# Another order of the on-chip buffers in an attention and feed-forward kernel

## The chip, the core and the metric

The kernel runs on one core of a Trainium2 chip. The metric is the device time of one execution in microseconds (us). SBUF, the on-chip memory, has 128 partitions, and a buffer takes the same bytes in each of them; "place" below always means a byte offset within a partition.

## The reference, cut to what matters

```python
xn = layernorm(x)                              # x: 8 batches x 2048 tokens x 256
q, k, v = split(xn @ Wqkv + bqkv)
qp, kp = elu(q) + 1, elu(k) + 1
kv = kp.T @ v ; ksum = sum(kp, tokens)         # per batch
attn = (qp @ kv) / (qp @ ksum + 1e-6)
z = layernorm(xn + attn) * g1 + b1
ffn = (silu(z @ Wg + bg) * (z @ Wu + bu)) @ Wd + bd     # hidden width 682
s = layernorm(z + ffn) * g2 + b2
out = x + s * silu(xn @ ternary(W).T * scale)
```

## The kernel before, in words

The tokens are cut into 32 groups of 512 (`TOK`), four tiles of 128 rows each. A program of one loop iteration per group is written out by hand for each engine (`TENSOR_JOBS`, `SCALAR_STEPS`, `VECTOR_STEPS`, `GPSIMD_STEPS`, and their fill and end forms); keys-values work runs up to five groups ahead of the feed-forward work, and semaphores alone tie the engines together. SyncE issues all transfers.

Most products are made in three parts (`parts3`): each operand is held as a high half and a low half (`_h`, `_l`, type fp32r), and high by high, low by high and high by low are added up in PSUM. Each product is one weight load of 128x128 (the left operand, L1278 and the helper `products`) and one pass of the right operand, the moving one, 512, 258 or 256 columns wide. The kinds that matter:

| job | weights (left) | moving (right) | columns |
|---|---|---|---|
| G, U, GU (`gate_or_up`) | `wgu_h`, `wgu_l` | `zT_h`, `zT_l` | 512 |
| Q | `wqk_h`, `wqk_l` | `xT_h`, `xT_l` | 512 |
| D (`Dn`), parts of h | `h_h`, `h_l` | `wd_h`, `wd_l` | 256 |
| D, last part | `ht` | `wd_h` | 256 |
| K | `xT_h`, `xT_l` | `wqk_h`, `wqk_l` | 256 |
| B | `xT_h`, `xT_l` | `tern` | 256 |
| XK | `xn_h`, `xn_l` | `kp_h`, `kp_l` | 256 |
| KV | `kv_h`, `kv_l` (as `xk_h`, `xk_l`) | `wv_h`, `wv_l` | 256 |
| N | `qp_h`, `qp_l` | `kv_h`, `kv_l` | 258 |
| warm | `ht` | `ht` | 512 |

The profile prints the moving operand and the weights of a row in alphabetical order, so that `bank<-kv_h,qp_h` is N with the weights `qp_h`. The warm products fill idle time at the start and are used by nothing.

The buffers are declared one after another (`sb(...)`), and each starts at the first multiple of 32 bytes behind the one before it; `ident`, the first, starts at a multiple of 128. So the five small buffers behind it and the small vectors and statistics further on decide where the large ones start. Steps within a buffer (chunks, tiles, 128 columns) are multiples of 512 bytes, except in `kv_h` and `kv_l`, whose two rows are `KVW` = 258 elements, 1032 bytes, long. Places of the operands modulo 128, worked out from the declarations:

| buffers | place modulo 128 before |
|---|---|
| `wqk_*`, `tern`, `wgu_*`, `wd_*`, `wv_*`, `xn_*`, `xT_*`, `kp_*` | 32 |
| `kv_h`: first row, second row | 32, 40 |
| `kv_l`: first row, second row | 64, 72 |
| `qp_h`, `qp_l` | 96 |
| `zT_*`, `h_*`, `ht` | 64 |

Of the kernel before, what the change touches and what calls it, by code (L numbers as in the profile page):

```python
# [211 lines left out]
def build_kernel(nc, x, wqkv, bqkv, wg, bg, wu, bu, wd, bd, g1, b1, g2, b2, wt, out):  # L212
# [10 lines left out]
    with ctx:  # L223
        def sb(name, shape, dt=f32):
            return ctx.enter_context(nc.sbuf_tensor(name, shape, dt))
# [3 lines left out]


        ident = sb("ident", [P, P])
        ones = sb("ones", [P, 1])
        one_zero = sb("one_zero", [P, 2])
        neg_half = sb("neg_half", [P, 1])
        less_h = sb("less_h", [P, 1])
        less_w = sb("less_w", [P, 1])

        wqk_h = sb("wqk_h", [P, DC, 2 * D], f32r)
        wqk_l = sb("wqk_l", [P, DC, 2 * D], f32r)
        tern = sb("tern", [P, DC, D], f32r)  # L240
# [3 lines left out]
        wd_h = sb("wd_h", [P, HC, D], f32r)  # L244
        wd_l = sb("wd_l", [P, HF, D], f32r)
        wv_h = sb("wv_h", [P, DC, D], f32r)
        wv_l = sb("wv_l", [P, DC, D], f32r)
        bvb = sb("bvb", [P, D])
        bk1b = sb("bk1b", [P, D])
        bq = sb("bq", [P, DC])  # L250
        bq1 = sb("bq1", [P, DC])
        nbq = sb("nbq", [P, DC])
        g1c = sb("g1c", [P, DC])
        b1c = sb("b1c", [P, DC])
        hb = sb("hb", [P, 2 * HC])
        hb0 = sb("hb0", [P, 2 * HC])
        hb1 = sb("hb1", [P, 2 * HC])
        tscale = sb("tscale", [P, 4])
# [6 lines left out]
        xn_h = sb("xn_h", [P, TILES, D], f32r)  # L265
        xn_l = sb("xn_l", [P, TILES, D], f32r)
        xT_h = sb("xT_h", [P, XT, DC, TOK], f32r)
        xT_l = sb("xT_l", [P, XT, DC, TOK], f32r)
        st = sb("st", [P, 3, TILES, 6])
        mv = sb("mv", [P, 3, TILES, 2])  # L270
        ve = sb("ve", [P, 3, TILES])
        rstd0 = sb("rstd0", [P, LN0, TILES])
        nmr0 = sb("nmr0", [P, LN0, TILES])
        kp = sb("kp", [P, KP, 2, D])
        ku = sb("ku", [P, KU, 2, D])
        kp_h = sb("kp_h", [P, TILES, D], f32r)
        kp_l = sb("kp_l", [P, TILES, D], f32r)
        ksum = sb("ksum", [P, 2, D])
        kv_h = sb("kv_h", [P, DC, KVW], f32r)
        kv_l = sb("kv_l", [P, DC, KVW], f32r)  # L280

        xq = sb("xq", [P, 3, TILES, D])
        qp = sb("qp", [P, DC, TOK])
        qp_h = sb("qp_h", [P, DC, TOK], f32r)
        qp_l = sb("qp_l", [P, DC, TOK], f32r)
        den = sb("den", [P, 2, 2])
        rstd1 = sb("rstd1", [P, TILES])
        nmr1 = sb("nmr1", [P, TILES])
# [4 lines left out]

        hs = sb("hs", [P, 2, TOK])
        h_h = sb("h_h", [P, HRING, TOK], f32r)
        h_l = sb("h_l", [P, HRING, TOK], f32r)

        ht = sb("ht", [P, TOK], f32r)  # L300
        norm2 = sb("norm2", [P, 2, TILES])
# [45 lines left out]
        def job_bank(kind, g, n):  # L347
            return bank[NUMBER[kind, g, n] % RING]
# [199 lines left out]
        def _(eng):  # L548
# [140 lines left out]
            for i in ITERATIONS:  # L689
                a, q, f, last = i + LEAD, i + 1, i, i - 1  # L690
                run_steps(order_of(i, FILL_GPSIMD, GPSIMD_STEPS, END_GPSIMD), {
                    "at": i,                    "xn_low": (a, xn_low), "sum_k": (a, sum_k), "z_g1": (f, z_g1), "tail_again": (f, tail_again), "last_gain": (last, last_gain), "last_offset": (last, last_offset),
                    "last_gate": (last, last_gate), "last_add": (last, last_add),
                    "end_terms": (f, end_terms),
                    "a_rstd": (a + 1, lambda g, p: first_rstd(p) if g == 0 else rstd(0, g, rstd0[:, g % LN0, :])),
                    "q_rstd": (q, lambda g, _: rstd(1, g, rstd1[:, :])),
                    "last_rstd": (last, lambda g, _: rstd(2, g, rstd2[:, :])), "setup_d_low": (a, setup_d_low), "setup_masks": (a, setup_masks)})


# [1 line left out]
        def _(eng):  # L701
# [223 lines left out]
        def _(eng):  # L925
# [348 lines left out]
        def _(eng):  # L1274
# [213 lines left out]
```

## Time and profile before

| | |
|---|---|
| median of 3 runs | 1224.95 us (1224.54 to 1226.43) |
| the profiled execution | 1226.01 us, span 1224.3 us |
| TensorE busy | 98% of the span |
| VectorE busy | 88% of the span |
| ScalarE busy | 78% of the span |
| GpSimd busy | 69% of the span |
| TensorE's granted clock, mean | 0.998 |

PE is TensorE's matmuls, PEld its weight loads, DVE VectorE, ACT ScalarE, POOL GpSimd. A matmul's duration in a row includes its way through the array, which overlaps the next one, so the time that a product takes of the engine is the distance from its start to the start of the next.

### The profile page before, as it was taken

The numbers are of one execution on the slowest core, as the hardware profiler recorded it, in microseconds if no ns is written. First come the engines' busy times: TensorE is split into PE (matmuls) and PEld (weight loads), VectorE is DVE, ScalarE is ACT, GpSimd is POOL, SyncE is SP. The second block draws the span as 40 slices with busy tenths as digits, with TensorE's granted clock in tenths as the row PEclk, the third lists the DMA queues.
The fourth block names the chain that finished last, engine by engine and source line by source line (L and its number), as shares of the span: only waits on it lengthen the run. The fifth ranks groups of instructions, "written<-read, shape, count | busy, mean of one in ns | idle before, by whom it ended". The sixth has DMA issues, their size and how long they took to land.

```text
span 1224.3 us, 24021 instructions
## 1 busy us (share of the span) xinstructions
PE 1205.6 (98%) x7550; PEld 1080.2 (88%) x7550; DVE 1081.3 (88%) x2467; ACT 953.4 (78%) x1557; POOL 842.6 (69%) x994
## 2 busy tenths in 40 slices
PE   8999999999999999999999999999999999999997
PEld 6889988999988999988999988999988999888886
DVE  6988999999999999999999999999999999777765
ACT  7787888777888777888778888778887778767753
POOL 3443787667687676787757787677776777666676
PEclk9999999999999999999999999999999999999999
DMA  7213432234432234432334432244432233222201
GB/s 215 76 46 87 121 105 69 87 104 121 122 103 70 87 105 121 121 104 70 86 104 120 116 109 70 72 119 122 121 95 58 94 118 104 69 70 67 73 18 35
DMA packets 137523, 115.61 MB, mean 94 GB/s; under 512 B 12339, under 2 KB 122293, under 8 KB 137398
## 3 DMA queue, kind: packets, MB, share of 16 engines
q1 hardware_dynamic: 137398, 114.08, 31.9%
q8 instruction: 62, 1.02, 0.3%
q14 instruction: 63, 0.52, 0.1%
HBM read 67.38 MB, written 46.67 MB: 93 GB/s over the span
## 4 chain that ended last, share of the span: by engine, by line
PE 90%; DVE 4%; issue 2%; DMA 1%; ACT 1%; POOL 1%; SPq 0%; DVEq 0%; POOLq 0%; ACTq 0%
PE bank L1278 64%; PE d_bank L1278 18%; PE xk_bank L1278 8%; DVE st L930 1%; DMA xa<-z_turned 1%; PE bank L1292 1%; DMA z_turned<-xa 1%; DVE rz L1062 0%; DVE zT_l L1093 0%; ACT rz L703 0%; DVE h_l L1113 0%; SPq L452 0%; DVE xa L1082 0%; POOL rstd L577 0%; ACT h_h L703 0%
## 5 line engine op out<-in xcount | busy, mean ns | idle before, releaser
L1278 PE MATMUL bank<-zT_h,wgu_h 128*128 128x512 f32 x704 | 278.5, 396 | 0.3 <-DVE rz L1062 0.3
L1278 PE MATMUL bank<-zT_l,wgu_h 128*128 128x512 f32 x704 | 278.5, 396 | 0.0
L1278 PE MATMUL bank<-zT_h,wgu_l 128*128 128x512 f32 x704 | 278.4, 395 | 0.0
L1278 PE MATMUL d_bank<-wd_h,h_h 128*128 128x256 f32 x640 | 180.6, 282 | 0.0
L1278 PE MATMUL d_bank<-wd_l,h_h 128*128 128x256 f32 x640 | 180.1, 281 | 0.0
L1278 PE MATMUL d_bank<-wd_h,h_l 128*128 128x256 f32 x640 | 180.1, 281 | 0.0
L1103 DVE SCALAR_TENSOR_TENSOR bank<-bank,hb,hs 128x512 f32<-128x512 f32 x160 | 118.2, 754 | 54.5 <-ACT hs L703 41.8
L1278 PEld LDWEIGHTS bank<-zT_l,wgu_h 128*128 128x128 f32 x704 | 132.3, 188 | 31.4
L703 ACT ACTIVATE h_h<-bank 128x512 fp32r<-128x512 f32 x160 | 95.7, 598 | 81.4 <-DVE bank L1103 81.3
L1278 PEld LDWEIGHTS bank<-zT_h,wgu_h 128*128 128x128 f32 x704 | 132.4, 188 | 25.9 <-DVE rz L1062 1.3
L1278 PEld LDWEIGHTS bank<-zT_h,wgu_l 128*128 128x128 f32 x704 | 132.9, 189 | 23.6
L703 ACT ACT_TABLE_LOAD x116 | 148.8, 1283 | 4.0 <-POOL wd_l L686 1.2
L703 ACT ACTIVATE hs<-bank,hb 128x512 f32<-128x512 f32 x192 | 128.1, 684 | 29.5 <-PE bank L1278 29.1
L600 POOL TENSOR_TENSOR ksum<-ksum,kp 128x256 f32<-128x256 f32 x120 | 107.7, 898 | 46.4 <-DVE kp L1029 43.1
L577 POOL TENSOR_TENSOR norm<-ve,neg_half 128x4 f32<-128x4 f32 x32 | 32.7, 1023 | 150.8 <-DVE ve L941 150.8
L1113 DVE TENSOR_TENSOR h_l<-bank,h_h 128x512 fp32r<-128x512 f32 x160 | 109.9, 687 | 23.7 <-ACT h_h L703 18.4
L703 ACT ACTIVATE rz<-rz,norm 128x256 f32<-128x256 f32 x124 | 74.2, 600 | 63.1 <-DVE norm L1139 63.1
L1278 PEld LDWEIGHTS d_bank<-wd_h,h_l 128*128 128x128 f32 x640 | 120.6, 189 | 2.8
L1278 PEld LDWEIGHTS d_bank<-wd_h,h_h 128*128 128x128 f32 x640 | 120.0, 187 | 3.4 <-DVE h_l L1113 0.5
L1278 PEld LDWEIGHTS d_bank<-wd_l,h_h 128*128 128x128 f32 x640 | 120.7, 189 | 0.0
L650 POOL TENSOR_TENSOR rz<-rz,g1b 128x256 f32<-128x256 f32 x128 | 117.4, 928 | 0.0
L610 POOL TENSOR_TENSOR rz<-rz,g2b 128x256 f32<-128x256 f32 x124 | 90.4, 739 | 34.9 <-ACT rz L703 34.9
(165 smaller groups left out, 3682.2 us busy)
## 6 DMA issues: line engine op xcount, KB each, us to landing
xq<-in_L_attn_x_dram SPq DMA_DIRECT2D x32, 512.0 KB, 5.9
xa<-in_L_attn_x_dram SPq DMA_DIRECT2D x31, 512.0 KB, 3.8
out_dram<-rz SPq DMA_DIRECT2D x31, 512.0 KB, 5.0
z_turned<-xa SPq DMA_DIRECT2D x120, 128.0 KB, 3.4
xa<-z_turned SPq DMA_DIRECT2D x30, 512.0 KB, 4.2
turned<-xa SPq DMA_DIRECT2D x108, 128.0 KB, 2.4
xa<-turned SPq DMA_DIRECT2D x27, 512.0 KB, 3.9
rz<-in_L_attn_Wg_dram SPq DMA_DIRECT2D x1, 640.0 KB, 5.7
```

The lines of the kernel that those rows point to most:

```text
L577: eng.tensor_tensor(dst, ve[:, k, :], neg_half[:, 0:1].to_broadcast([P, TILES]), ALU.pow).then_inc(S[f"rs{k}"], 1)
L600: eng.tensor_tensor(ksum[:, slot, :], ksum[:, slot, :], part, ALU.add).then_inc(S["ks"], 1)
L610: eng.tensor_tensor(row_, row_, g2b[:, :], ALU.mult).then_inc(S["a"], 1)
L650: eng.tensor_tensor(row_, row_, g1b[:, :], ALU.mult).then_inc(S["zg"], 1)
L703: return eng.activation(out_, in_, func, **kw).then_inc(S[name], 1)
L930: eng.bn_stats(st[:, k, t, :], rows).then_inc(S[f"bn{k}"], 1)
L1103: eng.scalar_tensor_tensor(out=hidden(g, c)[0:rows, :], in0=up, scalar=hb[0:rows, HC + c:HC + c + 1], in1=hs[0:rows, n % 2, :], op0=ALU.ad ...
L1113: eng.tensor_tensor(h_l[:, slot, :], hidden(g, c)[:, :], h_h[:, slot, :].bitcast(f32), ALU.subtract).then_inc(S["hl"], 1)
L1278: ins = eng.matmul(dst, left, right, start=first and n == 0, stop=last and n == len(pairs) - 1, **kw)
L1292: ins = eng.transpose(dst[:, c * D + t * P:c * D + (t + 1) * P], src[:, 2 * p + t, c * P:(c + 1) * P], ident[:, :])
```

## The change

The declarations are put into another order. The small buffers that split the large ones are gathered into a few (`consts`, `masks`, `norm1`, `vecs`) behind the operands, and views with the old names are cut from them. The rows of `kv_h` and `kv_l` get eight more elements than `D` instead of two, those of `qp_h` and `qp_l` eight more than `TOK`, and every use names the old width. Two small buffers, `hb` and `hb0`, stand between the halves of kv and of qp. No instruction is added, removed or moved in its engine's order, and no semaphore changes.

```diff
+SHIFT = 8
         ident = sb("ident", [P, P])
-        ones = sb("ones", [P, 1])
-        one_zero = sb("one_zero", [P, 2])
-        neg_half = sb("neg_half", [P, 1])
-        less_h = sb("less_h", [P, 1])
-        less_w = sb("less_w", [P, 1])
...
         wqk_h = sb("wqk_h", [P, DC, 2 * D], f32r)
         wqk_l = sb("wqk_l", [P, DC, 2 * D], f32r)
         tern = sb("tern", [P, DC, D], f32r)
+        wd_h = sb("wd_h", [P, HC, D], f32r)
+        wd_l = sb("wd_l", [P, HF, D], f32r)
+        kp_h = sb("kp_h", [P, TILES, D], f32r)
+        kp_l = sb("kp_l", [P, TILES, D], f32r)
+        kv_h = sb("kv_h", [P, DC, D + SHIFT], f32r)
+        hb = sb("hb", [P, 2 * HC])
+        kv_l = sb("kv_l", [P, DC, D + SHIFT], f32r)
+        xT_h = sb("xT_h", [P, XT, DC, TOK], f32r)
+        xT_l = sb("xT_l", [P, XT, DC, TOK], f32r)
+        h_h = sb("h_h", [P, HRING, TOK], f32r)
+        h_l = sb("h_l", [P, HRING, TOK], f32r)
+        ht = sb("ht", [P, TOK], f32r)
+        zT_h = sb("zT_h", [P, DC, TOK], f32r)
+        zT_l = sb("zT_l", [P, DC, TOK], f32r)
+        xn_h = sb("xn_h", [P, TILES, D], f32r)
+        xn_l = sb("xn_l", [P, TILES, D], f32r)
+        wv_h = sb("wv_h", [P, DC, D], f32r)
+        wv_l = sb("wv_l", [P, DC, D], f32r)
         NGU = (2 * HF + 1) * P
         wgu_h = sb("wgu_h", [P, DC, NGU], f32r)
         wgu_l = sb("wgu_l", [P, DC, NGU], f32r)
+        qp_h = sb("qp_h", [P, DC, TOK + SHIFT], f32r)
         hb0 = sb("hb0", [P, 2 * HC])
+        qp_l = sb("qp_l", [P, DC, TOK + SHIFT], f32r)
...
-                act(kv_h[:, c, :], job_bank("KV", g, c)[:, 0:KVW], ACT.Copy, "kvh")
+                act(kv_h[:, c, 0:KVW], job_bank("KV", g, c)[:, 0:KVW], ACT.Copy, "kvh")
...
-                    for pair in parts3(qp_h[:, c, s], qp_l[:, c, s], kv_h[:, c, :], kv_l[:, c, :])], "N")
+                    for pair in parts3(qp_h[:, c, s], qp_l[:, c, s], kv_h[:, c, 0:KVW], kv_l[:, c, 0:KVW])], "N")
```

Places modulo 128 after, by the same rule:

| buffers | place modulo 128 after |
|---|---|
| `wqk_*`, `tern`, `wd_*`, `kp_*` | 0 |
| `kv_h`, `kv_l`: first row, second row | 0, 32 |
| `xT_*`, `h_*`, `ht`, `zT_*`, `xn_*`, `wv_*`, `wgu_*` | 64 |
| `qp_h`, `qp_l`: first row, second row | 64, 96 |
| `bvb` and all behind it (`xa`, `xn`, `kp`, `ku`, `ksum`, `xq`, `qp`, `rz`, `sg`, `hs`) | 64 |

## Rows read from the trace of the kernel before

**Rows 1.** The page: span, and busy time of each engine over it.
```profile
span 1224.3 us, 24021 instructions
PE 1205.6 (98%) x7550; PEld 1080.2 (88%) x7550; DVE 1081.3 (88%) x2467; ACT 953.4 (78%) x1557; POOL 842.6 (69%) x994
```

**Rows 2.** Busy time by stretch: window, length, PE, PEld, DVE, ACT, POOL, clock, DMA.
```profile
200.00:1000.00 800.00, 799.90 (x5091) 723.41 (x5090) 742.31 (x1663) 653.03 (x1061) 585.82 (x673) 1.00 0.35 102
```

**Rows 3.** The chain that ended last, its longest pieces: start, length, what.
```profile
240.20 2.88 PE d_bank L1278 x24
...
368.86 18.84 PE bank L1278 x106
405.24 18.84 PE bank L1278 x106
```

**Rows 4.** Waits from 200 to 1000 us: total, times, longest.
```profile
DVE bank L1103 <- ACT hs L703: 27.1, 22, 1.4
...
PEld bank L1278 <- DVE h_l L1113: 1.0, 4, 0.5
```

**Rows 5.** Groups of PE's matmuls by form: count | busy us, mean ns | idle before.
```profile
L1278 PE MATMUL bank<-zT_l,wgu_h 128*128 128x512 f32 x704 | 278.5, 396 | 0.0
...
L1278 PE MATMUL d_bank<-wd_h,h_h 128*128 128x256 f32 x640 | 180.6, 282 | 0.0
...
L1278 PE MATMUL bank<-kv_h,qp_h 128*128 128x258 f32 x256 | 74.2, 290 | 1.7 <-DVE kv_l L1180 1.7
L1278 PE MATMUL bank<-wqk_h,xT_h 128*128 128x256 f32 x256 | 73.3, 286 | 0.1
...
L1278 PE MATMUL bank<-tern,xT_l 128*128 128x256 f32 x256 | 63.8, 282 | 0.0
...
L1278 PE MATMUL xk_bank<-kp_l,xn_h 128*128 128x256 f32 x224 | 63.3, 282 | 0.0
...
L1278 PE MATMUL bank<-xT_h,wqk_h 128*128 128x512 f32 x128 | 50.7, 396 | 0.1
...
L1278 PE MATMUL d_bank<-wd_h,ht 128*128 128x256 f32 x128 | 21.2, 287 | 0.0
```

**Rows 6.** Timeline of PE within one iteration: start us, duration us, what.
```profile
405.07 0.28 PE L1278 MATMUL bank<-wqk_h,xT_h 128*128 128x256 f32 x1
...
406.50 0.28 PE L1278 MATMUL bank<-kv_h,qp_h 128*128 128x258 f32 x1
...
406.85 0.30 PE L1278 MATMUL bank<-kv_h,qp_h 128*128 128x258 f32 x1
406.98 0.29 PE L1278 MATMUL bank<-kv_h,qp_l 128*128 128x258 f32 x1
...
409.43 0.39 PE L1278 MATMUL bank<-zT_h,wgu_h 128*128 128x512 f32 x1
...
416.45 0.28 PE L1278 MATMUL bank<-tern,xT_h 128*128 128x256 f32 x1
...
417.40 0.40 PE L1278 MATMUL bank<-zT_h,wgu_h 128*128 128x512 f32 x1
...
418.79 0.39 PE L1278 MATMUL bank<-xT_h,wqk_h 128*128 128x512 f32 x1
...
421.57 0.28 PE L1278 MATMUL bank<-tern,xT_h 128*128 128x256 f32 x1
```

**Rows 7.** Timeline of PE at two places of the fill: the warm products, merged.
```profile
12.64 1.29 PE L1278 MATMUL bank<-ht 128*128 128x512 f32 x5
...
69.13 0.85 PE L1278 MATMUL bank<-ht 128*128 128x512 f32 x3
69.82 0.28 PE L1278 MATMUL xk_bank<-kp_h,xn_h 128*128 128x256 f32 x1
```

**Rows 8.** DVE groups by form: count | busy us, mean ns | idle before, releasers.
```profile
L1113 DVE TENSOR_TENSOR h_l<-bank,h_h 128x512 fp32r<-128x512 f32 x160 | 109.9, 687 | 23.7 <-ACT h_h L703 18.4
...
L999 DVE TENSOR_TENSOR xT_l<-xa,xT_h 128x512 fp32r<-128x512 f32 x54 | 36.5, 676 | 0.0
```

More of the change, by code:

```diff
@@ L243, in build_kernel @@
         wgu_l = sb("wgu_l", [P, DC, NGU], f32r)
[L244 to L247, printed above, removed]
+        qp_h = sb("qp_h", [P, DC, TOK + SHIFT], f32r)
+        hb0 = sb("hb0", [P, 2 * HC])
+        qp_l = sb("qp_l", [P, DC, TOK + SHIFT], f32r)
+        hb1 = sb("hb1", [P, 2 * HC])
+        consts = sb("consts", [P, 4])
+        masks = sb("masks", [P, 2])
+        norm1 = sb("norm1", [P, 2, TILES])
+        norm2 = sb("norm2", [P, 2, TILES])
+        den = sb("den", [P, 2, 2])
+        tscale = sb("tscale", [P, 4])
+        vecs = sb("vecs", [P, 5, DC])
+        st = sb("st", [P, 3, TILES, 6])
+        mv = sb("mv", [P, 3, TILES, 2])
+        ve = sb("ve", [P, 3, TILES])
+        rstd0 = sb("rstd0", [P, LN0, TILES])
+        nmr0 = sb("nmr0", [P, LN0, TILES])
         bvb = sb("bvb", [P, D])
         bk1b = sb("bk1b", [P, D])
[L250 to L258, printed above, removed]
         g1b = sb("g1b", [P, D])
@@ L264, in build_kernel @@
         xn = sb("xn", [P, TILES, D])
[L265 to L273, printed above, removed]
         kp = sb("kp", [P, KP, 2, D])
         ku = sb("ku", [P, KU, 2, D])
-        kp_h = sb("kp_h", [P, TILES, D], f32r)
-        kp_l = sb("kp_l", [P, TILES, D], f32r)
         ksum = sb("ksum", [P, 2, D])
-        kv_h = sb("kv_h", [P, DC, KVW], f32r)
-        kv_l = sb("kv_l", [P, DC, KVW], f32r)
         xq = sb("xq", [P, 3, TILES, D])
         qp = sb("qp", [P, DC, TOK])
[L284 to L288, printed above, removed]
         rz = sb("rz", [P, RZ, TILES, D])
-        zT_h = sb("zT_h", [P, DC, TOK], f32r)
-        zT_l = sb("zT_l", [P, DC, TOK], f32r)
         sg = sb("sg", [P, SG, TILES, D])
         hs = sb("hs", [P, 2, TOK])
[L295 to L301, printed above, removed]
+        ones, one_zero, neg_half = consts[:, 0:1], consts[:, 1:3], consts[:, 3:4]
+        bq, bq1, nbq, g1c, b1c = (vecs[:, n, :] for n in range(5))
+        less_h, less_w = masks[:, 0:1], masks[:, 1:2]
+        rstd1, nmr1 = norm1[:, 0, :], norm1[:, 1, :]
         rstd2, nmr2 = norm2[:, 0, :], norm2[:, 1, :]
@@ L695, in _ @@
                     "a_rstd": (a + 1, lambda g, p: first_rstd(p) if g == 0 else rstd(0, g, rstd0[:, g % LN0, :])),
-                    "q_rstd": (q, lambda g, _: rstd(1, g, rstd1[:, :])),
+                    "q_rstd": (q, lambda g, _: rstd(1, g, rstd1)),
                     "last_rstd": (last, lambda g, _: rstd(2, g, rstd2[:, :])), "setup_d_low": (a, setup_d_low), "setup_masks": (a, setup_masks)})
@@ L776, in q_high @@
                     eng.wait_ge(S["N"], TILES * g)
-                act(qp_h[:, c, :], qp[:, c, :], ACT.Copy, "qph")
+                act(qp_h[:, c, 0:TOK], qp[:, c, :], ACT.Copy, "qph")
             def x_res(g, t):
@@ L1049, in q_low @@
                 eng.wait_ge(S["qph"], DC * g + c + 1)
-                eng.tensor_tensor(qp_l[:, c, :], qp[:, c, :], qp_h[:, c, :].bitcast(f32),
+                eng.tensor_tensor(qp_l[:, c, 0:TOK], qp[:, c, :], qp_h[:, c, 0:TOK].bitcast(f32),
                                   ALU.subtract).then_inc(S["qpl"], 1)
@@ L1071, in attn_norm @@
                     eng.wait_ge(S["z"], TILES * g)
-                eng.scalar_tensor_tensor(out=nmr1[:, :], in0=mv[:, 1, :, 0], scalar=-1.0,
-                                         in1=rstd1[:, :], op0=ALU.mult, op1=ALU.mult).then_inc(S["nm1"], 1)
+                eng.scalar_tensor_tensor(out=nmr1, in0=mv[:, 1, :, 0], scalar=-1.0,
+                                         in1=rstd1, op0=ALU.mult, op1=ALU.mult).then_inc(S["nm1"], 1)
             def z_turn(g, _=0):
@@ L1179, in kv_low @@
                     eng.wait_ge(S["kvh"], DC * (g // GPB) + c + 1)
-                    eng.tensor_tensor(kv_l[:, c, :], job_bank("KV", g, c)[:, 0:KVW],
-                                      kv_h[:, c, :].bitcast(f32), ALU.subtract).then_inc(S["kvl"], 1)
+                    eng.tensor_tensor(kv_l[:, c, 0:KVW], job_bank("KV", g, c)[:, 0:KVW],
+                                      kv_h[:, c, 0:KVW].bitcast(f32), ALU.subtract).then_inc(S["kvl"], 1)
             def setup_bk():
```

## The prediction

> **What bounds the kernel now.** The page comes first: TensorE is busy for 98% of the span, VectorE, the next, for 88% [rows 1]. An average hides stages, so the middle was read as a stretch of its own: between 200 and 1000 us TensorE is busy for 799.90 of 800 us, VectorE for 742.31 [rows 2]. The clock there is the full one (1.00, 2.4 GHz) in that same row. The chain of waits agrees: its long pieces are TensorE's, and the same piece comes back after 405.24 - 368.86 = 36.38 us, one iteration [rows 3]. TensorE hardly waits for anyone (1.0 us in those 800, [rows 4]). So the time is the number of products by the distance between their starts, and what is to be asked is whether the places of the operands set that distance.
>
> The timeline gives the distances [rows 6]. K: 12 products from 405.07 to 406.50, 119 ns each. N: 24 from 406.50 to 409.43, 122 ns. G and U: 30 from 409.43 to 416.45, 234 ns. B: 8 from 416.45 to 417.40, 119 ns. Q: 12 from 418.79 to 421.57, 232 ns. D: 24 in 2.88 us, 120 ns [rows 3].
>
> **The change part by part.** Nothing is issued that was not issued before, so no instruction, wait or transfer has a price of its own. What can change is the distance between products, and the duration of other engines' instructions.
>
> *Gate and up products.* Before, their weights stand at 32 and z at 64 (modulo 128); after, both at 64. The trace has products of the same width and type with both operands at 64: the warm ones. Five of them take 1.29 us, and taking off the last one's 0.39 leaves four distances in 0.90, 225 ns, by rounding 223 to 227 [rows 7, 6]. In the second place three warm products stand before a product of XK, whose weights are at 32: 69.13 to 69.82 is 230 ns each [rows 7], between the two values, as it should be if a load of weights at 32 beside a stream at 64 is what costs. I take 227, the upper end. Against it: the warm products load the same weights again and again, early in the fill. Bounds: 0 (234 stays) and 9 ns (225). There are 3 x 704 products [rows 5], so 2112 x 7 = 14.8 us. A loss is not excluded by any mechanism that I know; the nearest price for one is N's below.
>
> *N.* Its distances are not equal: the one from 406.85 to 406.98 is 130 ns, against 117 (406.50 to 406.85 is three products) [rows 6]. The long distances, two of each six, have the second row of `kv_h` as the moving operand, which begins 8 bytes behind a multiple of 32; after, it begins at 32. The 3 x 256 products [rows 5] hold 256 of that kind, and 256 x 9 ns is 2.3 us. If the first rows, at 0 beside weights at 64, gain what the next paragraph takes for its products, that is 384 x 6 = 2.3 us more. Sum 4.6.
>
> *The 256-wide products (D, K, B, XK, KV).* Before, every moving operand stands at 32; the weights at 32, or 64 in D, and the distance is 119 to 120 either way [rows 3, 6]. After, the moving operand is at a multiple of 64 in all and the weights too, but 64 bytes apart modulo 128. No row shows a 256-wide product with both at multiples of 64. Upper bound: the cost goes with the columns, and half of 227 is 113.5, a gain of 6. Lower bound: nothing (119.5 stays), or, on the other side, N's 130, a loss of 10. I take 6, from the warm products, the only rows in which both operands are so placed. The count is 3 x 640 + 128 (D), 3 x 256 (K), 2 x 256 (B), 3 x 224 (XK) [rows 5], 4000: 24 us. KV's are few and left out.
>
> *Q.* 3 x 128 products [rows 5] go from 32 and 32 to weights at 0, x at 64. From 232 to 227 is 5 ns, 1.9 us; bounds 0 and 7 ns.
>
> A rule of the Trainium skill speaks against these terms: "SBUF — State Buffer", note on SBUF "cachelines" in the section on the DMA port swizzle, has lines of 16 bytes, and by those every operand here but the second rows of kv already starts on a line. Then N's 2.3 us would be all. The trace doesn't side with it: starts at 32 and at 64 are both on such lines, and 234 stands against 225 [rows 6, 7].
>
> *The other engines.* Their buffers move too, mostly from 32 or 96 to 64. VectorE's low half of h, with operands at 64, takes 687 ns, and that of x, at 32, 676 [rows 8]; so they cost 0, with 11 ns either way as the bound. These are two of about 75 instructions in an iteration (1663 in 800 us, [rows 2]); 11 ns on 20 long ones would be 0.2 us of an engine that has room.
>
> **What is late next.** Sum of TensorE's terms: 14.8 + 4.6 + 24 + 1.9 = 45.3 us, over 32 groups about 1.4 us each, from some 36.9 (one iteration in four is longer by the keys-values work: 800 us hold 21.7). VectorE is busy for 742.31 / 21.7 = 34.2 us of these 36.9. With 35.5 it would have 1.3 us of idle time left, where it now waits 1.2 us an iteration (27.1 / 21.7) for ScalarE's silu alone [rows 2, 4]. Those waits hang on TensorE's products and move forward with them, but not all of them will fit: in an order written out by hand, some product will find its operand late. I give back a quarter, 11 us. A gain of 34 us on the profiled execution's 1226.01 gives 1192; it stood 1 us above the median of the runs, so 1191 against 1224.95.
>
> **The rivals.**
> - *Only the gate and up products gain* (and N's second rows): the 256-wide ones and Q stay because for so short a stream the load of the next 128 columns of weights is as long as the stream. For it: D, with weights at 64, is no faster than K with 32 [rows 3, 6]. Against: no row has such a product's moving operand at 64. 14.8 + 2.3 = 17 us, no idle time of VectorE used up: 1208.
> - *VectorE takes over earlier*: half of the 45 us is given back, 1203.
> - *The places don't matter*: warm products are quick because they reload the same weights, not for their place. For it: G with weights at 32 (234) and Q with its moving operand at 32 (232) are nearly alike. Left is N's 2.3 us, 1222.6, which is 0.19%. This is also the rule on lines of 16 bytes.
> - *Slower*: weights 64 bytes from the stream clash with it. This holds for all 256-wide products after. At the price of N's long distances (10 ns) it costs 40 us on 4000 products, less the 14.8 of gate and up and 2.3: 1248. It decides from about 4 ns a product (17.1 us / 4000). Against: N's first three products are 64 apart in two of three (`qp` at 96, `kv_h` at 32) and take 117 ns.
>
> **How the numbers follow.** Forecast (both widths gain) 50%, its own range 1180 to 1200; only gate and up 22%; VectorE takes over 10%; places don't matter 10%; slower 8%. The two next cases lie at 1203 and 1208, with some 6 us about them for unknown sizes, so 1178 to 1214 holds the first three less their edges, 8 in 10. Faster by over 0.2% (2.4 us, about what a measurement of this kernel can tell from no change): the first three and a share of the fourth, 85%; within it 7%; slower 8%.
>
> **What would show it.** Distances in the timeline of the changed kernel: G and U at 227 instead of 234; K, B, D and XK at 113 to 114 instead of 119; all N products alike, none at 130; VectorE's busy share in 200 to 1000 us at 95% or more, and small waits of TensorE on VectorE. If G and U stay at 234 the first term is wrong, and with it the reading of the warm products; if K and D stay at 119 the first rival holds; if TensorE's products are as said and the iteration is longer than 36 us, VectorE took over.

## The result, and the profile after

The kernel after takes 1212.78 us (median of 4 runs, 1211.86 to 1213.07), the kernel before 1225.42 beside it: ratio 0.9897, 95% interval [0.9881, 0.9912]. It is faster by 12.6 us, where the prediction had 34; the time lies inside the range. The profiled execution took 1213.05 us. Of all executions told below, one, the profiled one of `by32`, was disturbed (3042.83 us); it is left out of that kernel's time, and the kernel has no row in the table.

The page's span and busy times, and the middle as one stretch (window, length, PE, PEld, DVE, ACT, POOL, clock, DMA), answer to [rows 1, 2]:
```profile
span 1211.3 us, 24021 instructions
PE 1191.9 (98%) x7550; PEld 1069.5 (88%) x7550; DVE 1081.7 (89%) x2467; ACT 952.8 (79%) x1557; POOL 843.9 (70%) x994
```
```profile
200.00:1000.00 800.00, 799.88 (x5127) 723.31 (x5126) 749.92 (x1687) 657.26 (x1069) 593.21 (x680) 1.00 0.35 102
```
TensorE still bounds it: full clock, busy for all of the 800 us, but 5127 products start in that time instead of 5091. VectorE does the same work (1081.7 us against 1081.3) in less time.

The chain (start, length, what) has the pieces of [rows 3], 18.57 us for 18.84 and 2.83 for 2.88, and a period of 583.22 - 547.33 = 35.89 us for 36.38:
```profile
237.43 2.83 PE d_bank L1268 x24
...
547.33 18.57 PE bank L1268 x106
583.22 18.57 PE bank L1268 x106
```

The timeline of PE in one iteration (start, duration), for [rows 6]:
```profile
401.11 0.28 PE L1268 MATMUL bank<-wqk_h,xT_h 128*128 128x256 f32 x1
...
402.53 0.28 PE L1268 MATMUL bank<-kv_h,qp_h 128*128 128x258 f32 x1
...
405.40 0.40 PE L1268 MATMUL bank<-zT_h,wgu_h 128*128 128x512 f32 x1
...
406.79 0.42 PE L1268 MATMUL bank<-zT_h,wgu_h 128*128 128x512 f32 x1
407.06 0.40 PE L1268 MATMUL bank<-zT_h,wgu_l 128*128 128x512 f32 x1
407.29 0.39 PE L1268 MATMUL bank<-zT_l,wgu_h 128*128 128x512 f32 x1
407.52 0.39 PE L1268 MATMUL bank<-zT_h,wgu_h 128*128 128x512 f32 x1
```
K: 12 products in 1.42 us, 118 ns each. N: 24 in 2.87, 120. In G and U one distance is 270 ns (406.79 to 407.06), the next two 230. A single series proves little, so the means over the whole kernel are needed.

The table below has them, for this kernel and for the experiments told further on. From the starts of all products in the timeline the distance to the next start was taken, sorted by kind; distances over 250 ns (512 columns), 140 (258) or 135 (256) were counted apart as waits, with what they exceed 230, 120 or 119 ns by. "Sum" is the mean of each kind times its count: 2112 G and U, 384 Q, 2048 D, 768 K, 512 B, 672 XK, 768 N, and 96 KV, which have no column of their own.

| kernel | G/U | Q | D | K | B | XK | N | sum, us | waits: count, us |
|---|---|---|---|---|---|---|---|---|---|
| before | 233.3 | 231.8 | 119.7 | 118.7 | 119.0 | 119.1 | 122.0 | 1164.3 | 59, 9.9 |
| **after** | 229.4 | 233.4 | 117.9 | 117.6 | 118.0 | 118.1 | 119.6 | 1148.7 | 95, 13.2 |
| gu_only | 232.1 | 231.5 | 118.2 | 118.8 | 118.5 | 118.6 | 121.6 | 1157.6 | 66, 10.6 |
| same | 229.3 | 227.5 | 119.7 | 119.9 | 119.2 | 119.4 | 119.9 | 1153.6 | 78, 11.5 |
| g128 | 232.5 | 233.0 | 117.7 | 117.6 | 117.7 | 117.8 | 119.9 | 1154.7 | 80, 11.6 |
| rows | 229.5 | 233.3 | 117.9 | 117.6 | 117.9 | 118.0 | 119.3 | 1148.5 | 98, 15.9 |
| turned | 228.2 | 230.1 | 117.4 | 117.2 | 116.9 | 117.7 | 120.6 | 1143.5 | 94, 14.5 |
| light | 229.0 | 233.2 | 117.8 | 117.6 | 118.0 | 118.1 | 119.5 | 1147.8 | 60, 9.9 |
| g192 | 229.9 | 230.8 | 114.5 | 114.7 | 116.5 | 115.7 | 120.6 | 1138.2 | 121, 19.3 |
| n192 | 228.0 | 229.9 | 117.3 | 117.1 | 117.0 | 117.7 | 120.1 | 1142.6 | 94, 14.1 |
| g192_light | 229.6 | 233.0 | 114.3 | 114.3 | 116.9 | 115.5 | 120.5 | 1137.6 | 60, 11.2 |
| a192 | 230.5 | 233.2 | 117.7 | 117.3 | 117.7 | 117.8 | 119.8 | 1150.3 | 79, 11.8 |

After against before: products 1164.3 - 1148.7 = 15.6 us shorter, waits 3.3 us longer. From the start of the first matmul to that of the last it is 1212.4 us before and 1199.4 after, 13.0 less; 15.6 - 3.3 = 12.3 leaves 0.7 for the products not in the table.

Where the waits are: the waits of PEld from 200 to 1000 us (total, times, longest), beside [rows 4]:
```profile
PEld bank L1268 <- DVE h_l L1103: 3.1, 10, 0.4
...
PEld bank L1268 <- DVE rz L1052: 1.9, 8, 0.5
```
The products that need h_l waited 1.0 us before and wait 3.1 now. Two groups by form (count, busy us, mean ns, idle before) answer to [rows 8]; 687 ns is unchanged, and 677 was 676:
```profile
L1103 DVE TENSOR_TENSOR h_l<-bank,h_h 128x512 fp32r<-128x512 f32 x160 | 110.0, 687 | 23.3 <-ACT h_h L693 17.5
...
L989 DVE TENSOR_TENSOR xT_l<-xa,xT_h 128x512 fp32r<-128x512 f32 x54 | 36.6, 677 | 0.0
```

### The profile page after: what moved, and what is told of

Read it like the earlier page. It is cut to its first block, busy times and chain, and to the rows that moved or that the text cites. A ratio compares the mean times of both kernels' runs of the same rounds, so it can differ in the third digit from the quotient of the medians.

```text
span 1211.3 us, 24021 instructions
## 1 busy us (share of the span) xinstructions
PE 1191.9 (98%) x7550; PEld 1069.5 (88%) x7550; DVE 1081.7 (89%) x2467; ACT 952.8 (79%) x1557; POOL 843.9 (70%) x994
## 4 chain that ended last, share of the span: by engine, by line
PE 90%; DVE 5%; issue 2%; DMA 2%; ACT 1%; POOL 1%; SPq 0%; DVEq 0%; POOLq 0%; ACTq 0%
PE bank L1268 63%; PE d_bank L1268 18%; PE xk_bank L1268 8%; DVE st L920 1%; DMA xa<-z_turned 1%; DMA z_turned<-xa 1%; PE bank L1282 1%; DVE rz L1052 0%; DMA turned<-xa 0%; POOL norm L567 0%; DVE bank L1093 0%; ACT rz L693 0%; DVE xn L972 0%; DVE mv L927 0%; DVE zT_l L1083 0%
## 5 line engine op out<-in xcount | busy, mean ns | idle before, releaser
L1268 PE MATMUL bank<-zT_h,wgu_l 128*128 128x512 f32 x704 | 274.3, 390 | 0.0
L693 ACT ACTIVATE rz<-rz,norm 128x256 f32<-128x256 f32 x252 | 140.5, 595 | 59.8 <-DVE norm L1129 59.8
L567 POOL TENSOR_TENSOR norm<-ve,consts 128x4 f32<-128x4 f32 x64 | 72.8, 1138 | 153.7 <-DVE ve L931 153.5
L1093 DVE SCALAR_TENSOR_TENSOR bank<-bank,hb,hs 128x512 f32<-128x512 f32 x160 | 117.9, 754 | 53.8 <-ACT hs L693 41.9
L1268 PEld LDWEIGHTS d_bank<-wd_h,h_h 128*128 128x128 f32 x640 | 119.8, 187 | 3.1 <-DVE h_l L1103 0.5
L1268 PEld LDWEIGHTS d_bank<-wd_l,h_h 128*128 128x128 f32 x640 | 120.1, 188 | 0.0
L640 POOL TENSOR_TENSOR rz<-rz,g1b 128x256 f32<-128x256 f32 x128 | 118.1, 933 | 0.0
```

The source lines that it names most:

```text
L567: eng.tensor_tensor(dst, ve[:, k, :], neg_half[:, 0:1].to_broadcast([P, TILES]), ALU.pow).then_inc(S[f"rs{k}"], 1)
L640: eng.tensor_tensor(row_, row_, g1b[:, :], ALU.mult).then_inc(S["zg"], 1)
L693: return eng.activation(out_, in_, func, **kw).then_inc(S[name], 1)
L1093: eng.scalar_tensor_tensor(out=hidden(g, c)[0:rows, :], in0=up, scalar=hb[0:rows, HC + c:HC + c + 1], in1=hs[0:rows, n % 2, :], op0=ALU.ad ...
L1268: ins = eng.matmul(dst, left, right, start=first and n == 0, stop=last and n == len(pairs) - 1, **kw)
```

## The experiments

They are told in the order in which they ran, in which one theory gave way to the next. `d` is the **distance of places**: the weights' place less the moving operand's.

**Places alone** (`places`). A kernel that computes nothing of the reference: series of 24 products (more in the first) that go round three blocks of weights and two of moving columns, every operand constant. The output is written with ones. Weights stand 128 bytes further on than the letters say, modulo 256 (`wa` at 128, `ma` at 0).
```diff
+PLACES = {"a": 0, "b": 8, "c": 16, "d": 24, ...}      # in elements of 4 bytes
+SERIES += [(w, m, 512, 24) for w in "abcd" for m in "abcd"]
+SERIES += [(w, m, 256, 24) for w in "abcd" for m in "abcd"]
...
+                    left = W[w][:, (k % 3) * P:(k % 3 + 1) * P]
+                    right = M[m][:, (k // 3 % 2) * 512:(k // 3 % 2) * 512 + cols]
+                    ins = eng.matmul(bank[n // 6 % 4][:, 0:cols], left, right, start=True, stop=True)
```

> A kernel of its own that computes nothing of the reference: only products of two constant fp32r buffers, 24 in a row for each pair of places modulo 128 of weights and moving operand (0, 32, 64, 96 each; also 8, 16, 40, 48, 72) at 512, 384, 258, 256 and 128 columns, and a constant written to the output. Theory 1 (two limits): a 512-wide product is set by its stream and takes 227 ns where both operands are at multiples of 64, 232 to 235 where one is not; a 256-wide one is set by the load of the next weights, so it is 118 at best and 128-wide ones take the same 118. Rival 2 (the relation decides): what counts is the distance of the two places modulo 128, so 512-wide pairs at 32 and 32 are as quick as 64 and 64, and pairs 64 apart are slower, 233 at 0 and 64. Rival 3 (the column rule of the prediction): 256-wide takes 113 with both at multiples of 64 and 128-wide 57 to 110. After a product of another width in front (258, 2, 130, 200, 384), a series at 64 and 64 either settles at 227 whatever comes first, or stays at about 230, which would be what the gate and up products show after the change.

Whole series in the timeline of PE, merged. The distance between starts is the length less the last product's own (0.39 or 0.28), over the count less one:
```profile
77.63 5.67 PE L68 MATMUL bank<-ma,wc 128*128 128x512 f32 x24
...
44.04 5.75 PE L68 MATMUL bank<-mc,wa 128*128 128x512 f32 x24
```
```profile
127.94 2.90 PE L68 MATMUL bank<-mc,wa 128*128 128x256 f32 x24
...
144.79 2.99 PE L68 MATMUL bank<-ma,wc 128*128 128x256 f32 x24
```
The two letters exchanged give two answers: 229 and 233 ns with 512 columns, 113.9 and 117.8 with 256. `mc,wa` has `d` = 64 and `ma,wc` 192. So it isn't that both are at multiples of 64 (all four series have that), nor how far apart the places are without their sign, and the order that is quick for one width is slow for the other. None of the theories put down beforehand holds as it stands. The 32 series of these two widths leave a rule on `d` with its sign: two pairs that stand off the multiples of 64, weights at 224 and moving at 32 (`d` = 192), and weights at 160 and moving at 96 (`d` = 64), settle at the same quick distances.
```profile
105.54 5.65 PE L68 MATMUL bank<-mb,wd 128*128 128x512 f32 x24
...
142.06 2.90 PE L68 MATMUL bank<-md,wb 128*128 128x256 f32 x24
```
The next question is the period.

**Gate and up alone** (`gu_only`), in the kernel before: four small buffers move round `wgu_*`, which goes from 32 to 64 modulo 128.
```diff
         NGU = (2 * HF + 1) * P
+        bq = sb("bq", [P, DC])
         wgu_h = sb("wgu_h", [P, DC, NGU], f32r)
         wgu_l = sb("wgu_l", [P, DC, NGU], f32r)
+        bq1 = sb("bq1", [P, DC])
+        nbq = sb("nbq", [P, DC])
+        g1c = sb("g1c", [P, DC])
```

> The kernel before with one part of the change: the gate and up weights at 64 modulo 128, z's place; all else stays at 32. Theory 1: G and U at 229 to 230 ns instead of 234, 2112 products, so 9 us less, 1216; D, K, B, XK stay at 119 to 120 and N's second rows at 130. If the 256-wide products gained nothing in the full change, this is worth all 12.6 us: 1213.

1220.06 us (1219.22 to 1220.38), ratio 0.9952 [0.9938, 0.9966]. G and U go from 233.3 to 232.1, not to 227: 2112 x 1.2 = 2.5 us. More, 2048 x 1.5 = 3.1 us, comes from D, whose `wd_*` moved by 128 bytes, from `d` = 160 to 32, which the prediction's table of places modulo 128 doesn't show at all. So places have to be kept at least modulo 256; `scan` and `g128` below show that this is enough.

**Everything 32 bytes on** (`by32`). One buffer ahead of all operands; every distance between them stays, and none but the second rows of kv and qp is at a multiple of 64 any more.
```diff
         ident = sb("ident", [P, P])
+        consts = sb("consts", [P, 4])
         wqk_h = sb("wqk_h", [P, DC, 2 * D], f32r)
...
-        consts = sb("consts", [P, 4])
```

> The kernel after with one small buffer put ahead of the operands, so that every operand is 32 bytes further on, at 32 or 96 modulo 128, and all distances between them are as after. Rival 2 (relation): as after, 1213. Theory 1 (multiples of 64): G and U back to 232 to 235, 256-wide ones back to 119 to 120, so 1222 to 1226.

1213.03 us (three runs, 1212.63 to 1213.79), ratio 0.9898 [0.9883, 0.9913]: the same as after. Multiples of 64 are worth nothing; the time goes with the distances. There is no trace to read its products from, so this rests on the time, and on the two pairs shown under `places`.

**All operands at one place** (`same`). The kernel after with the operands of TensorE at 192 modulo 256, so `d` = 0 for all kinds but N and KV: `kv_l` and `qp_l` stand 128 bytes further on, and the products that use one of them have `d` = 128.
```diff
         ident = sb("ident", [P, P])
+        consts = sb("consts", [P, 4])
+        masks = sb("masks", [P, 2])
...
         kv_l = sb("kv_l", [P, DC, D + SHIFT], f32r)
+        hb1 = sb("hb1", [P, 2 * HC])
         xT_h = sb("xT_h", [P, XT, DC, TOK], f32r)
```

> The kernel after with all operands at 64 modulo 128 (three small buffers moved), so that D, K, B, XK, N and Q have weights and moving operand at one place instead of 64 bytes apart. Theory 1: the 256-wide ones stay at 118; Q goes from 234 to 227 to 230, 384 products, 2 us less: 1211. Rival 2 with a cost for 64 apart: the 256-wide ones fall to 114, as the prediction had it, 15 us or more less: 1195 to 1200. If 64 apart is what brought them to 118, they go back to 119 to 120 and it is 1217.

1215.92 us (1215.58 to 1217.32), ratio 0.9923 [0.991, 0.9935], 3.1 us slower than after: products 4.9 us longer, waits 1.7 shorter. Q goes from 233.4 to 227.5 ns, and D, K and XK go up to 119.4 to 119.9. Each width has its own good distance.

**The scan** (`scan`). The first kernel again (nothing of the reference computed), with places every 32 bytes, from 0 to 480 for the weights, and then for the moving operand.
```diff
-PLACES = {"a": 0, "b": 8, "c": 16, "d": 24, ...}
+PLACES = {chr(97 + n): 8 * n for n in range(16)}
```

> Products of constant fp32r buffers alone, as in places, nothing of the reference. The moving operand stands at 0 modulo 512 and the weights at every multiple of 32 up to 480, at 512, 256 and 258 columns, then the weights at 0 and the moving operand at every multiple of 32; a few places in between (48, 56, 72, 80, 184, 200). New theory, from places: the distance from the moving operand to the weights counts modulo 256, not modulo 128, and not whether the places are multiples of 64. Then a 256-wide product takes 113 ns at 64 and at 320, 118 at 192 and at 448, 119 at 128 and 384; a 512-wide one 229 at 192 and 448, 233 to 234 at 64, 128, 320 and 384; and at 0, which places did not hold and where the gate and up products stand after the change, 227 or 230. With the weights at 0 and the moving operand at m the same numbers at 256 - m. Rival 2a (modulo 512): 64 and 320 differ. Rival 1 (multiples of 64 count): 32, 96, 160 and 224 are all alike and worse, and 64 and 192 are alike.

512 columns, 30 products a series, the moving operand at 0, weights at 32 (`wb`), 64 and so on to 256 (`wi`), in the timeline of PE:
```profile
52.16 7.15 PE L70 MATMUL bank<-ma,wb 128*128 128x512 f32 x30
59.15 7.16 PE L70 MATMUL bank<-ma,wc 128*128 128x512 f32 x30
66.16 7.18 PE L70 MATMUL bank<-ma,wd 128*128 128x512 f32 x30
73.17 7.13 PE L70 MATMUL bank<-ma,we 128*128 128x512 f32 x30
80.14 7.17 PE L70 MATMUL bank<-ma,wf 128*128 128x512 f32 x30
87.15 7.04 PE L70 MATMUL bank<-ma,wg 128*128 128x512 f32 x30
94.03 7.17 PE L70 MATMUL bank<-ma,wh 128*128 128x512 f32 x30
101.03 7.00 PE L70 MATMUL bank<-ma,wi 128*128 128x512 f32 x30
```
256 columns: weights at 0 (`wa`), 64, 160 and 192; then weights at 0 and the moving operand at 64 (`mc`), 192 (`mg`) and 320 (`mk`):
```profile
156.74 3.03 PE L70 MATMUL bank<-ma,wa 128*128 128x256 f32 x24
...
162.44 2.99 PE L70 MATMUL bank<-ma,wc 128*128 128x256 f32 x24
...
170.93 3.04 PE L70 MATMUL bank<-ma,wf 128*128 128x256 f32 x24
173.81 2.99 PE L70 MATMUL bank<-ma,wg 128*128 128x256 f32 x24
...
278.59 2.89 PE L70 MATMUL bank<-mc,wa 128*128 128x256 f32 x24
...
289.85 2.89 PE L70 MATMUL bank<-mg,wa 128*128 128x256 f32 x24
...
301.12 2.99 PE L70 MATMUL bank<-mk,wa 128*128 128x256 f32 x24
```
The settled distances, which are the means over the later products of each series (from about the twelfth on):

| `d` modulo 256 | 0 | 32 | 64 | 96 | 128 | 160 | 192 | 224 |
|---|---|---|---|---|---|---|---|---|
| 512 columns, ns | 226.7 | 233.4 | 233.4 | 234.3 | 232.4 to 233.5 | 233.4 | 228.7 | 233.3 |
| 256 columns, ns | 120 | 118.2 | 117.8 or 113.4 | 117.1 | 118.4 to 118.8 | 120.2 | 117.8 or 113.4 | 117 to 118 |
| 258 columns, ns | 121.1 | 120.2 | 120.8 | 119.9 | 122.3 | 120.2 | 119.0 | 119.8 |

It comes back after 256 bytes, whichever operand is moved. Two facts stand in it that the edits of the kernel so far had not shown: 512 columns have two good distances, 0 and 192; and with 256 columns two distances, 64 and 192, have two answers each, `mc,wa` (192) quick and `ma,wg` (192) and `mk,wa` (192) not.

Off the multiples of 32 the rule is looser: at `d` = 48 a 256-wide series takes 122.7 ns in `places` (`ma,wf`, from 227.73 us) and 118.3 in `scan` (`ma,wq`). And 258-wide products have two answers at 192 as well: the pair `mb,wd` of `places` takes 121.9 ns from 167.50 us and 119.2 from 184.75.

Now the kernels' table can be read. Before, `d` was 96 for G and U, 128 for Q, K, B and XK, 160 for D, and 64 and 32 for the first rows of N. After, it is 0 for G and U, 64 for Q, 64 and 192 for N, and 192 for D, K, B and XK, and these have 117.8, the slower answer of 192.

**Gate and up at 128** (`g128`). If the period were 128, 0 and 128 would be one distance. The kernel after with `d` = 128 for G and U and the rest as it was.
```diff
+        consts, masks, norm1, norm2                     # moved here from behind hb1
         wgu_h = sb("wgu_h", [P, DC, NGU], f32r)
         wgu_l = sb("wgu_l", [P, DC, NGU], f32r)
+        den, tscale, vecs                               # moved here, too
         qp_h = sb("qp_h", [P, DC, TOK + SHIFT], f32r)
```

> The kernel after with the gate and up weights 128 bytes further on (192 modulo 256, 64 modulo 128 as before; z at 64 modulo 256). If places count modulo 128, nothing changes: 1213. If distances count modulo 256, G and U go from a distance of 0 to 128, from 229.3 to 232.8 ns (scan), 2112 products: 7.4 us more, 1220.

1217.97 us (1217.09 to 1218.46), ratio 0.9941 [0.9928, 0.9953]. G and U take 232.5 ns, as the scan has it for 128, and not the 229.4 of `d` = 0. 256 it is.

**Rows of the old length** (`rows`), with small buffers put so that all first rows keep their places:
```diff
-        kv_h = sb("kv_h", [P, DC, D + SHIFT], f32r)
+        kv_h = sb("kv_h", [P, DC, KVW], f32r)
...
-        qp_h = sb("qp_h", [P, DC, TOK + SHIFT], f32r)
+        qp_h = sb("qp_h", [P, DC, TOK], f32r)
```

> The kernel after without the longer rows of kv and qp: rows of 258 and 512 elements again, so kv's second rows start 8 bytes behind a multiple of 128, all first rows and all other operands where they are after. The prediction's term: N's products on the second rows go back to 130, 256 of them by 9 to 12 ns: 2.3 to 3 us more, 1215.5. If the distance modulo 256 is all there is, no place near 64 or 192 costs more than 2 ns and the time is within 1 us of 1213.

1213.8 us (1212.77 to 1215.6), ratio 0.9909 [0.9895, 0.9922]; N takes 119.3 ns, with longer rows 119.6. The longer rows are worth nothing that can be measured. Before, the long distances were the fourth and fifth of each six (129.6 and 126.1 ns on average); here the second rows begin 8 bytes behind a multiple of 32 again, and those two take 122.1 and 117.2. So N's 2.4 ns came from the first rows' places.

**The groups turned round** (`turned`). The 256-wide products' `d` is 64 instead of 192, Q's is 192, and that of G and U is 0 as after.
```diff
+        consts, masks, norm1, norm2                     # moved
         wqk_h = sb("wqk_h", [P, DC, 2 * D], f32r)
...
+        den, tscale, vecs                               # moved
         xT_h = sb("xT_h", [P, XT, DC, TOK], f32r)
```

> The kernel after with the moving operands of the 256-wide products (and kv) moved by 128 bytes, so that their weights stand 64 bytes ahead of them modulo 256 instead of 64 behind, and Q's weights 192 instead of 64 ahead of x. Theory B: K, B, D and XK go from 117.8 to 113.4, 4000 products, 17.6 us less, and Q from 234 to 229, 2 us less, some of it lost to VectorE: 1193 to 1200. Theory A: only Q gains for certain, 1211, and the 256-wide ones where their entry happens to be right.

1209.82 us (1208.95 to 1210.52), ratio 0.9875 [0.986, 0.989]. Q gains 3.3 ns, 1.3 us; the 256-wide products gain 0.4 to 1.1 ns, not the 4 that the quick answer would give. These means are mixtures: of the series of at least eight, 9 of 92 of D, 8 of 62 of K, 1 of 28 of XK and 25 of 63 of B have the quick answer.

**What decides between 117.8 and 113.4** (`entry`). The third of the kernels that compute nothing of the reference: four pairs of places, each as a series of 18 products of 256 columns behind 23 different lead-ins.
```diff
+BEFORE = [(("a", "a", 512, n),) for n in (6, ..., 11)] + [(("e", "a", 256, n),) for n in (5, ..., 9)]
+BEFORE += ...                # 256 and 258 wide at other distances; 512 x12 and one odd width
+for w, m in (("c", "a"), ("g", "a"), ("a", "c"), ("a", "g")):
+    for first in BEFORE:
+        SERIES += [*first, (w, m, 256, 18)]
```

> Products of constant fp32r buffers alone, nothing of the reference. In scan a 256-wide series at a distance of 64 or 192 modulo 256 kept one of two distances from start to start all through, 113.4 or 117.8 ns. Here four such pairs (weights at 64 or 192 with the moving operand at 0, and the other way round) each follow 23 different lead-ins: 512-wide, 256-wide and 258-wide series of several lengths and single narrow products. Theory A (the entry decides): each pair shows both values, and which one depends on the lead-in. Theory B (the order of the two buffers decides): the value goes with the pair, 117.8 where the weights are at 64 or 192 and the moving operand at 0, 113.4 the other way round.

The timeline of PE, for one pair of places (`ma,wc`, 64) behind eleven products of 512 columns and behind five and six of 256:
```profile
64.78 2.68 PE L67 MATMUL bank<-ma,wa 128*128 128x512 f32 x11
67.30 2.29 PE L67 MATMUL bank<-ma,wc 128*128 128x256 f32 x18
69.42 0.75 PE L67 MATMUL bank<-ma,we 128*128 128x256 f32 x5
70.01 2.29 PE L67 MATMUL bank<-ma,wc 128*128 128x256 f32 x18
72.13 0.87 PE L67 MATMUL bank<-ma,we 128*128 128x256 f32 x6
72.85 2.21 PE L67 MATMUL bank<-ma,wc 128*128 128x256 f32 x18
```
The last 18 take 2.21 us where the same 18 took 2.29: one product more ahead of them, and the distance is 113.5 instead of 118.2. Over all: 11 of 23 quick with weights at 64 and moving at 0, 8 of 23 with moving at 192 (both `d` = 64), 7 of 23 with moving at 64, 0 of 23 with weights at 192 (both `d` = 192). Behind 512-wide products alone, of whatever number, none of the 24 is quick. So the answer is taken at the entry of a series and kept. That the order of the buffers in memory decides, fell here. What in the lead-in decides is not settled: one product more changes it. These kernels change the output bank every six products, and a lead-in shifts that round too; but it doesn't decide alone, for with weights at 64 and moving at 0 series that begin at the same point of the round of 24 products have given both answers, at four such points.

**Less work for VectorE** (`light`). The kernel after with statistics over half of each row.
```diff
-                eng.bn_stats(st[:, k, t, :], rows).then_inc(S[f"bn{k}"], 1)
+                eng.bn_stats(st[:, k, t, :], rows[:, 0:P]).then_inc(S[f"bn{k}"], 1)
```

> The kernel after, with the layer norms' statistics taken over 128 of the 256 columns (the computation is changed in this), so that VectorE has 12 shorter instructions an iteration, some 1.5 us less of its 34. In the kernel after the shorter distances add up to some 15 us and 13 came out, with more waits of TensorE for VectorE. If those waits are VectorE's lack of room, they go: 2 to 3 us less, 1210 to 1211. If they come from the written order and not from room, the time stays at 1213 within 1 us.

1208.26 us (1207.62 to 1208.35), ratio 0.9862 [0.9847, 0.9876]. The middle (columns as above) and the one row left of PEld's waits:
```profile
200.00:1000.00 800.00, 800.00 (x5144) 727.06 (x5143) 736.38 (x1698) 662.56 (x1073) 586.13 (x683) 1.00 0.35 102
```
```profile
PEld bank L1268 <- issue: 0.6, 4, 0.2
```
Waits for VectorE are gone, from 13.2 to 9.9 us in the table, which is the figure of before. Of the 4.5 us gained, 3.3 are those and 0.9 the products. (The edit leaves out half of the statistics, so it is a test and not a version to use.)

**Gate and up at 192** (`g192`). `turned`, with `d` = 192 for G and U: it costs them a little against 0 and changes the lead-in of whatever follows them.
```diff
+        rstd0, nmr0                                     # moved, to the groups turned round
         wgu_h = sb("wgu_h", [P, DC, NGU], f32r)
         wgu_l = sb("wgu_l", [P, DC, NGU], f32r)
+        hb1 = sb("hb1", [P, 2 * HC])
         qp_h = sb("qp_h", [P, DC, TOK + SHIFT], f32r)
```

> turned with the gate and up weights 192 instead of 0 ahead of z modulo 256. By scan a long series takes 228.8 at 192 and 226.7 at 0, but in turned G and U take 228.2 on average, since they come in from other products. Distance alone: 229 to 230, 2 us more, 1212. If this also changes how the 256-wide products behind them come in, and puts some of them to 113.4 instead of 117.8, up to 10 us less, 1200 to 1208.

1208.07 us (1207.26 to 1208.65), ratio 0.9859 [0.9843, 0.9875]; its interval lies below that of after. It computes the whole reference and is the quickest version found. The timeline of PE, twelve D and twelve K:
```profile
397.21 0.28 PE L1268 MATMUL d_bank<-wd_h,h_h 128*128 128x256 f32 x1
...
398.57 0.62 PE L1268 MATMUL d_bank<-wd_h,ht 128*128 128x256 f32 x4
399.02 0.28 PE L1268 MATMUL bank<-wqk_h,xT_h 128*128 128x256 f32 x1
...
400.38 0.28 PE L1268 MATMUL bank<-kv_h,qp_h 128*128 128x258 f32 x1
```
399.02 to 400.38 is 113.3 ns each, and so is 397.21 to 398.57: the quick answer, in the kernel itself, in 82 of the 92 series of D, 44 of 62 of K, 45 of 63 of B and 25 of 28 of XK. Against before the products are 1164.3 - 1138.2 = 26.1 us shorter, but the run only 16.6 (1224.71 beside it); the waits are 19.3 - 9.9 = 9.4 us longer. Its middle and waits (views as above):
```profile
200.00:1000.00 800.00, 797.91 (x5146) 717.75 (x5145) 752.35 (x1698) 660.05 (x1073) 596.68 (x684) 1.00 0.35 102
```
```profile
PEld bank L1268 <- DVE h_l L1103: 6.2, 19, 0.6
...
PEld bank L1268 <- DVE rz L1052: 3.8, 16, 0.7
```
Before, h_l cost 1.0 us here; now it costs 6.2, at a VectorE busy for 94% of the stretch.

**N at another distance** (`n192`), in `turned`: `ve` and `hb1` ahead of `kv_h`, `mv` and `tscale` ahead of `kv_l`, others so that the rest keep their places.
```diff
+        ve, hb1                                         # moved
         kv_h = sb("kv_h", [P, DC, D + SHIFT], f32r)
         hb = sb("hb", [P, 2 * HC])
+        mv, tscale                                      # moved
         kv_l = sb("kv_l", [P, DC, D + SHIFT], f32r)
```

> turned with N's operands all at a distance of 192 modulo 256 (before a mixture of 64 and 192). By scan a 258-wide product takes 119.0 at 192 and 120.8 at 64; in turned N takes 121.3. 768 products by 2 ns: 1.5 us less, 1208.3; unless G and U, which follow N, come in worse and lose their 227.

1209.3 us (1208.95 to 1209.74), ratio 0.9871 [0.9857, 0.9886], not to be told from `turned`. N: 120.1 against 120.6 ns, 0.4 us.

**Both: quick products and less for VectorE** (`g192_light`). `g192` with the statistics of `light`.
```diff
-                eng.bn_stats(st[:, k, t, :], rows).then_inc(S[f"bn{k}"], 1)
+                eng.bn_stats(st[:, k, t, :], rows[:, 0:P]).then_inc(S[f"bn{k}"], 1)
```

> g192 with the layer norms' statistics over 128 of 256 columns, as in light (the computation is changed in this). In g192 the distances add up to 26 us less than before, 17 came out, and TensorE's long distances hold 9 us more than before. If VectorE's room is all that stands between, these 9 go and the time is 1224.7 - 26 = 1198 to 1200. If the new waits come from the written order, light's 4 to 5 us are all there is: 1203 to 1204.

1199.75 us (1198.83 to 1200.01), ratio 0.9789 [0.9775, 0.9802]. D, K, B and XK as in `g192` (Q is 2.2 ns slower, which nothing here explains), waits 19.3 to 11.2 us, and these 8.1 are nearly all of the 8.3 us between the two. So with room on VectorE the program keeps nearly the whole gain of the products: 25.7 of 26.7 us.

**Gate and up at 192, the others as after** (`a192`; `d` = 192): is it the lead-in alone?
```diff
+        rstd0, nmr0                                     # moved, in the kernel after
         wgu_h = sb("wgu_h", [P, DC, NGU], f32r)
         wgu_l = sb("wgu_l", [P, DC, NGU], f32r)
+        hb1 = sb("hb1", [P, 2 * HC])
         qp_h = sb("qp_h", [P, DC, TOK + SHIFT], f32r)
```

> The kernel after with the gate and up weights alone moved by 192 bytes, to a distance of 192 from z modulo 256; the 256-wide products keep their distance of 192. Theory (what comes before decides, whichever of 64 and 192 the pair has): D and K fall from 117.8 to 113.4 as in g192, Q stays at 233, VectorE takes most of it: 1208 to 1211. Rival (a distance of 64 is needed too): D and K stay at 117.8, G and U at 229 to 230: 1213.

1213.52 us (1212.07 to 1213.92), ratio 0.99 [0.9886, 0.9914]. D and K stay at 117.7 and 117.3 ns. The lead-in of `g192` does next to nothing for products at 192 (7 of 245 series quick, 4 in the kernel after); here it takes both, that lead-in and 64.

## Why the prediction was wrong, and where it was right

- **What bounds the kernel, and that places set the distance of products**: right. TensorE's 15.6 us are the gain, and the clock was full before and after. Instructions, their order and VectorE's durations (687 ns, then 687) gave nothing, as put.
- **The quantity**: wrong, and the step from which the rest follows: "I take 6, from the warm products, the only rows in which both operands are so placed". The prediction tabled places modulo 128 and read the warm products as "both operands at 64". They have one buffer as both operands, so what they showed was `d` = 0, and no row of before could tell the two readings apart. `same` can't either: it has Q at 227.5 ns with both operands at 64 modulo 128, as in the warm products. What decides is `places`, where both operands at multiples of 64 take 229 or 233 ns by the sign of `d`, and `by32`, where G, U, Q, D, K, B and XK have no operand at such a multiple and the time is that of after. `scan` and `g128` show that the period is 256.
- **G and U, 14.8 us**: the mechanism holds (`d` is 0 after, as in the warm products), the size is 8.2 us, 233.3 to 229.4. The step that failed is "I take 227" for every product. 227 is what a long series comes down to, in the scan after up to ten products. In the kernel after, the products from the eleventh of a series on take 227.3 ns (755 of them; before, 233.7), the first ten of the longer series 230.1, and those in series of six, which are 696 of the 2112, 231.1. The 230 ns of the three warm products at 69.13, which the prediction put down to weights at another place, are the start of such a series: 224, 231 and 235.
- **The 256-wide products, 24 us**: the step that cost the prediction most. Measured 5.9 us (D 3.7, K 0.8, B 0.5, XK 0.7, KV 0.2): TensorE's terms were put at 45.3 us and came to 15.6, and 18.1 of the missing 29.7 are here. "The cost goes with the columns, and half of 227 is 113.5" fails twice: at `d` = 0, where 512 columns take 227, a 256-wide product takes 120 ns, nearly its worst among the multiples of 32 (`same`, `scan`), and after, it stands at 192, which can give 113.4 and did so in 4 of 245 series. `g192` shows that the kernel can have 113.4 in most series, at places that the prediction had no view of; that a figure near its 113.5 exists doesn't bear out the halving, which has no place for two answers.
- **N, 4.6 us**: measured 1.8, and its second-row part is refuted: `rows` puts the second rows back at 8 bytes and stays at 119.3 ns, without the long distances.
- **Q, a gain of 1.9 us**: 231.8 to 233.4, a loss of 0.6. At `d` = 64 there is nothing to win with 512 columns; `same` and `turned` show 227.5 at 0 and 230.1 at 192.
- **A quarter given back to VectorE**: right in kind and about in size, 3.3 of 15.6 us (21%), taken away by `light`. In `g192` it is 9.4 of 26.1. The wait is the one named, for h_l; VectorE's share of the stretch is 93.7%, under the 95% put down, as the iteration shrank less.
- **The rivals**: the nearest was "only the gate and up products gain", 1208: its time is close, its reason is not, as G and U gave 8.2 and the 256-wide ones 5.9. "The places don't matter" and "64 apart clashes" are out; at 512 columns, though, 64 apart is one of the places without gain.

The lines of 16 bytes that the Trainium skill, "SBUF — State Buffer", has in the section on the DMA port swizzle don't order these times either: 233.4 and 226.7 ns both have all operands on such lines.

Left open: what in a lead-in puts a 256-wide series at 113.4 or at 117.8, why weights at 192 and moving at 0 were quick in none of 23 lead-ins, and through what part of the chip the distance works. All of it is what was measured, not a mechanism.

## What to carry to other kernels

Where TensorE bounds a kernel of fp32r products as it does here, the place of its weights less the place of its moving operand, modulo 256 bytes, is worth up to 3% of a product at 512 columns (226.7 to 234.3 ns) and up to 6% at 256 (113.4 to 120.2), at multiples of 32 bytes: 0 or 192 for 512 columns, 64 or 192 for 256. Each kind has to be measured in its own program, since 256-wide series can fall on either of two distances. A row in which both operands are one buffer tells of one distance only and not of alignment. What TensorE wins has to be matched by the engine behind it: VectorE, busy for 93.7% (after) and 94.0% (`g192`) of the stretch, took back 21% and 36% of it.

## What the runs showed of the hardware that was not expected

- The period of 256 bytes in the difference of the two places, with 512-wide products from 226.7 to 234.3 ns and 256-wide ones from 113.4 to 120.2 at multiples of 32 bytes.
- The two settled distances of 256-wide products at one and the same pair of places, 113.4 and 117.8 ns, chosen by as little as one product more ahead of them.
- With 128 columns the place was worth nothing at the three distances tried, 128, 160 and 192: 111.5 to 111.9 ns, hardly less than the 113.4 of twice the columns. Two series in the timeline of PE in the kernel `places`, with `d` = 128 and 192, show it; they start 2.68 us apart, 24 products of 111.7 ns. 384-wide ones take 173.3 ns at `d` = 192 and 175.6 to 176.8 at the two others tried, 128 and 160.
```profile
190.25 2.84 PE L68 MATMUL bank<-mb,wb 128*128 128x128 f32 x24
192.93 2.84 PE L68 MATMUL bank<-ma,wc 128*128 128x128 f32 x24
```
